# Turning from one batch to the next: a separate buffer for the first 64 tokens, no special order for the turning head

## The reference

```python
xn = _layernorm(x, axis=-1)
# attention
q = (x @ Wq + bq).reshape(b, h, t, dh)                        # no transpose of (t, h)
k = (x @ Wk + bk).reshape(b, t, h, dh).transpose(0, 2, 3, 1)
v = (x @ Wv + bv).reshape(b, t, h, dh).transpose(0, 2, 1, 3)
logits = jnp.einsum('bhtd,bhds->bhts', q, k) * scale
weights = jax.nn.softmax(logits + mask, axis=-1)
out = jnp.einsum('bhts,bhsd->bhtd', weights, v).transpose(0, 2, 1, 3).reshape(b, t, h * dh)
return out @ Wo + bo
# whole
x = x + attn(xn, ...) + ffn(xn, w_gate, w_shared_up, w_shared_down, w_up, w_down)
```

## Time and profile before

| | us |
|---|---|
| median of 3 runs | 1817.88 |
| lowest, highest of the 3 | 1813.98, 6824.79 |
| profiled execution, whole time | 1822.72 |
| its span, first to last instruction | 1821.0 |
| PE busy | 1690.2 (93% of the span) |
| DVE, POOL, ACT busy | 1368.7, 1122.1, 1085.7 |
| mean granted clock of PE | 0.956 of full speed |

### The profile page before, as it was taken

One profiled execution on the slowest core, in us unless ns is written; L12 is line 12 of the kernel. 1 busy time (PEld: TensorE's weight loads), 2 busy tenths in 40 slices (PEclk: granted clock), 3 DMA queues, 4 the chain that ended last, 5 costly groups with the idle time before them and its releaser, 6 DMA issues. The chain is left out here.

```text
span 1821.0 us, 49686 instructions
## 1 busy us (share of the span) xinstructions
PE 1690.2 (93%) x19217; PEld 1315.9 (72%) x19217; DVE 1368.7 (75%) x3128; ACT 1085.7 (60%) x2347; POOL 1122.1 (62%) x1006
## 2 busy tenths in 40 slices
PE   4699999999999999999986779999998999999997
PEld 3477767777777777777665667777776777777775
DVE  8677777777677777777663446888888888888885
ACT  2566666665566666666661227666666666666664
POOL 0257757776676777776660006777777677777763
PEclk7799999999999999999997669999999999999998
DMA  9377667765656665656656656778988789898976
GB/s 372 112 152 131 121 120 128 135 112 101 120 94 101 96 106 95 96 95 101 115 99 160 206 160 119 138 142 141 164 140 159 122 141 165 139 143 136 163 129 113
DMA packets 686658, 245.04 MB, mean 135 GB/s; under 512 B 637456, under 2 KB 674721, under 8 KB 685536
## 3 DMA queue, kind: packets, MB, share of 16 engines
q1 hardware_dynamic: 657472, 197.83, 61.6%
q0 software_dynamic: 18432, 33.64, 7.7%
q10 hardware_dynamic: 10528, 10.49, 1.8%
HBM read 57.11 MB, written 50.46 MB: 59 GB/s over the span
## 5 line engine op out<-in xcount | busy, mean ns | idle before, releaser
L485 POOL TENSOR_TENSOR prob<-prob 128x128 f16<-128x128 f32 (+7 forms) x512 | 653.0, 1280 | 576.1 <-ACT prob L874 569.2
L867 ACT ACTIVATE prob<-prob,nmax 128x128 f32<-128x128 f32 (+7 forms) x512 | 396.8, 775 | 530.4 <-DVE prob L1312 514.3
L708 PE MATMUL ps_s<-kT,qT 128*128 128x512 f16 (+3 forms) x2304 | 459.7, 327 | 4.3 <-DVE prob L1312 4.3
L723 PE MATMUL ps_o<-probT,vh 128*128 128x256 f16 (+1 forms) x3840 | 428.3, 265 | 7.2 <-DMA probT<-prob 7.2
L1312 DVE TENSOR_SCALAR_CACHE_REDUCE prob<-ps_s,neg_scale 128x128 f32<-128x128 f32 (+7 forms) x512 | 412.2, 809 | 14.3 <-PE ps_s L710 10.6
L723 PEld LDWEIGHTS ps_o<-probT,vh 128*128 128x128 f16 x3840 | 368.7, 99 | 53.5 <-issue 9.1
L874 ACT CAST prob<-prob 128x128 f16<-128x128 f32 (+7 forms) x512 | 341.5, 667 | 2.3
L708 PEld LDWEIGHTS ps_s<-kT,qT 128*128 128x128 f16 x2304 | 201.9, 98 | 144.7 <-issue 4.3
L1341 DVE SCALAR_TENSOR_TENSOR resid<-ps_y,yscale,resid 128x256 f32<-128x256 f32 x512 | 223.0, 477 | 11.6 <-PE ps_y L737 5.8
L737 PE MATMUL ps_y<-wo,oT 128*128 128x256 f16 x1536 | 210.6, 273 | 22.2 <-DVE oT L1327 20.4
L599 PEld LDWEIGHTS ps_t<-xT,wq 128*128 128x128 f16 x6144 | 205.1, 100 | 24.6 <-issue 9.8
(11 more groups left out here) (182 smaller groups left out, 1651.6 us busy)
## 6 DMA issues: line engine op xcount, KB each, us to landing
dispatched<-zeros SPq DMA_DIRECT2D x16, 512.0 KB, 14.1
probT<-prob SPq DMA_TRANSPOSE x512
ex<-dispatched SPq DMA_DIRECT2D x16, 512.0 KB, 4.3
expert_out<-eo ACTq DMA_DIRECT2D x16, 512.0 KB, 3.7
eup<-in_L_ffn_w_up_dram SPq DMA_DIRECT2D x64, 64.0 KB, 2.1
dispatched<-xn,slot_idx POOLq DMA_INDIRECT x192
xn_columns<-xnth SPq DMA_DIRECT2D x24, 128.0 KB
got<-expert_out,slot_idx POOLq DMA_INDIRECT x192
```

The source lines that it names most:

```text
L485: pool.tensor_tensor(low_cols(j), prob_cols(j).rearrange("p (r k) -> p r k", k=P), high_cols(j), ALU.subtract).then_inc(p_low, 1)
L708: pe.matmul(s_cols(j, lo, hi), qT[:, u, a, j * P:(j + 1) * P], kT[:, u, c, lo:hi], start=(n == 0), stop=(n == 2 and hi < w))
L723: mm = pe.matmul(ps_o[:, lo:2 * P], vh[:, u, a, r * D:(r + 1) * D], probT[:, PT_AT[c] + 2 * r + s, lo:], start=(r + n == 0), stop=(r == 2 ...
L867: nc.scalar.activation(prob_cols(j), prob_cols(j), ACT.Exp, bias=nmax[:, j:j + 1], scale=-1.0, accum_out=rsum[:, i % 2, j:j + 1]).then_inc ...
```

## The change

The order of the turning head is made that of every other head: `turn` and all its branches on PE, ACT and DVE are deleted. A buffer `xT_first` (64 KB) is added for the first 64 tokens of a batch. `load_first(b)` fills it with one DMA, listed on SP in the head before the turning one (14, 30, 46), between the transposes of block 6 and block 7. It waits for the stored columns of the batch and for the queries of the previous batch's first head, which were the last to read the buffer. The first queries of a batch read `xT_first` in place of `xT`. `load_xT` moves from ahead of block 1 to ahead of block 2 of the turning head, still waits for `v_done`, and brings all 1024 tokens in two halves of 512 (two DMAs of 256 KB each), each half with a semaphore of its own; each half of the first keys waits for its half of the tokens.

```diff
+            def load_first(b):
+                sp.wait_ge(xt_stored, 32 * NC * b)
+                sp.wait_ge(q_done, 2 * H * (b - 1) + 2)
+                sp.dma_start(xT_first[:], xnT_d[:, :, :, b * T:b * T + TPH]).then_inc(xT_head, 16)
+
             def load_xT(b):
-                sp.wait_ge(xt_stored, 32 * NC * b)
                 sp.wait_ge(v_done, 2 * H * b)
-                for n in range(2):
-                    sp.dma_start(xT[:, n, :, 0:TPH], xnT_d[:, n, :, b * T:b * T + TPH]).then_inc(xT_head, 16)
-                for n in range(2):
-                    sp.dma_start(xT[:, n, :, TPH:], xnT_d[:, n, :, b * T + TPH:(b + 1) * T]).then_inc(xT_in, 16)
+                for r in range(2):
+                    for n in range(2):
+                        sp.dma_start(xT[:, n, :, r * 512:(r + 1) * 512], xnT_d[:, n, :, b * T + r * 512:b * T + (r + 1) * 512]).then_inc(xT_in[r], 16)
...
                     for j in range(TB):
-                        if j == 1 and turn(i, i < B * H - 1):
+                        if j == TB - 1 and i % H == H - 2 and i < B * H - 2:
+                            load_first(i // H + 1)
+                        if j == 2 and i % H == H - 1 and i < B * H - 1:
                             load_xT(i // H + 1)
                         transpose_probs(i, j)
...
                 elif h == 0 and half == 0:
-                    pe.wait_ge(xT_head, 32 * (i // H))
+                    pe.wait_ge(xT_head, 16 * (i // H))
...
-                                           xT[:, c, k, h * TPH:(h + 1) * TPH], start=False, stop=(n + k == 3 and m % (H // 2) == H // 2 - 1))
+                                           xT_first[:, c, k, :] if i and h == 0 else xT[:, c, k, h * TPH:(h + 1) * TPH], start=False, stop=(n + k == 3 and m % (H // 2) == H // 2 - 1))
...
-                elif h == 0 and half == 0:
-                    pe.wait_ge(xT_in, 32 * (i // H))
+                elif i and h == 0:
+                    pe.wait_ge(xT_in[half], 32 * (i // H))
...
                     scores(i, 1)
-                    if turn(i, more):
-                        project_v(i, 0, more)
-                        project_v(i, 1, more)
-                    elif more:
+                    if more:
                         project_q(i + 1, 0)
                         project_q(i + 1, 1)
...
                     scores(i, 3)
-                    if turn(i, more):
-                        project_q(i + 1, 0)
-                        project_q(i + 1, 1)
-                    else:
-                        project_v(i, 0, more)
-                        project_v(i, 1, more)
+                    project_v(i, 0, more)
+                    project_v(i, 1, more)
```

More of the change, by code:

```diff
@@ L210, in causal_attention_with_moe @@
         xT_head = sem("xT_head")
-        xT_in = sem("xT_in")
+        xT_in = [sem(f"xT_in{n}") for n in range(2)]
         q_done = sem("q_done")
@@ L264, in causal_attention_with_moe @@
         xT = sb("xT", [P, 2, KC, T], F16)
+        xT_first = sb("xT_first", [P, 2, KC, TPH], F16)
         nmax = sb("nmax", [P, TB])
@@ L318, in late_part @@
             return i // 2 - 1 if i % 2 == 0 and 2 <= i <= ROWS else -1
-        def turn(i, more):
-            return more and i % H == H - 1
         def p_uses(i, j):
@@ L577, in project_q @@
                 elif h == 0 and half == 0:
-                    pe.wait_ge(xT_head, 32 * (i // H))
+                    pe.wait_ge(xT_head, 16 * (i // H))
                 if not fresh:
-                    if h == 0:
-                        pe.wait_ge(v_low, 2 * i - 1 + half)
-                    else:
-                        pe.wait_ge(k_low, 2 * i - 1 + half)
+                    pe.wait_ge(k_low, 2 * i - 1 + half)
                 if half == 0 and odd_part(i - 2) >= 0:
@@ L606, in project_k @@
                     pe.wait_ge(wsplit[1], 1)
-                elif h == 0 and half == 0:
-                    pe.wait_ge(xT_in, 32 * (i // H))
-                if fresh or h == 0:
+                elif i and h == 0:
+                    pe.wait_ge(xT_in[half], 32 * (i // H))
+                if fresh:
                     pe.wait_ge(q_low, 2 * i + half + 1)
@@ L629, in project_v @@
                     pe.wait_ge(wsplit[2], 1)
-                if more and not turn(i, more):
+                if more:
                     pe.wait_ge(q_low, 2 * i + half + 3)
@@ L647, in free_second_bank @@
             def free_second_bank(i):
[L648 to L651, removed]
+                pe.wait_ge(v_low, 2 * i + 2)
             def transpose_rows(i, p):
@@ L939, in attention @@
                     old, more = i > i0, i < i1 - 1
-                    swap = turn(i, more)
                     if odd_part(i) >= 0:
@@ L964, in attention @@
                     softmax_exp(i, 1)
[L965 to L968, removed]
+                    if more:
                         high_q(i + 1, 0)
                     high_probs(i, 1)
-                    if more and not swap:
+                    if more:
                         high_q(i + 1, 1)
@@ L979, in attention @@
                     softmax_exp(i, 3)
[L980 to L984, removed]
+                    high_v(i, 0)
+                    high_v(i, 1)
                     high_probs(i, 3)
-                    if swap:
-                        high_q(i + 1, 1)
                     softmax_exp(i, 4)
@@ L1373, in mixed @@
                         return max(0, min(NT * (TOPK + 1), TB * (i - i0) + j - MIX_LAG + 1)) if mixing else 0
-                    swap, even, odd, late = turn(i, more), even_part(i), odd_part(i), late_part(i)
+                    even, odd, late = even_part(i), odd_part(i), late_part(i)
                     block_max(i, 0)
@@ L1419, in attention @@
                         low_weights(2)
[L1420 to L1425, removed]
+                    low_v(i, 0)
+                    low_v(i, 1)
                     if odd >= 0:
```

## The result

| | before | changed |
|---|---|---|
| median, us | 1817.49 (6 runs) | 1826.29 (6 runs) |
| lowest and highest of the changed kernel's runs | | 1823.59, 1830.04 |
| ratio to before, 95% interval | | 1.0065 [1.0052, 1.0078] |
| profiled execution, us (span) | 1822.72 (1821.0) | 1830.04 (1828.3) |

The changed kernel is 0.65% slower. That is within the 2% band, but its 95% interval leaves out 1: some 9 us by the medians, 11.8 by the ratio, 7.3 between the two profiled executions. Measured again on another chip, in the last set of experiments, the ratio was 1.0067 [1.0049, 1.0086]. (One of the six runs of before took 6824.79 us and is no part of the ratio.)

What follows compares the result with a forecast made beforehand. PE, busy 93% of the span, was taken as the bound. Stalls of 17.5 us plus 6.1 for the clock against 15.5 before gave +8.1; +7 was taken, from 1817.9 to 1825, range 1813 to 1832, likeliest 1820 to 1829.

Steps and rivals of the forecast that it cites:

- Where PE asks, and where SP stands: First queries of a batch, after scores 1: SP issues the load 1.4 to 1.7 us after PE begins to wait.
- How long the load takes: Load of `xT_first` on SP's queue: stalls of 10.4 us as lower bound, 17.5 us as upper, the upper taken.
- the load's packets start only behind these: SP's queue: load moves after block 6's 448 KB transpose, needs another 1.3 us, lands at 465.1, 883.3 and 1402.3.
- The clock: Matmuls after each turn's stall run at a lower clock: 2.0 us each, 6.1 in all; 1.4 each for stalls of 3.4 to 3.6.
- The keys: First keys of the turning head: their half of the tokens lands 1.5 us before they ask, at no cost.
- The held transposes: SP holds transposes of blocks 2 and 3 behind the load of `xT`: hidden with 2 us to spare, no cost.
- The sum: Three turns: 15.5 us before, 23.6 after, +8.1 by the upper bound, −0.9 by the lower; +7 taken.
- The overtaking load: Rival on SP's queue: the load slips past the transpose, −0.9 us, 1817; chance 0.22.
- The early load: Rival at the turns: the load arrives before PE asks, turns become ordinary heads, −15.5 us, 1802; chance 0.06.
- The forecast's stall with a new one behind it: Rival: first keys or ACT's block 5 also wait, one to two us a turn, +10 to +14, about 1830; chance 0.12.

Runs made afterwards that it cites:

- e_early: Changed kernel with the 64-token load listed one head earlier on SP (heads 13, 29, 45), with the shorter wait for stored columns: 1805.99 us, 0.9924 of before.
- e_late: Changed kernel with the 64-token load one transpose later, behind that of block 7 of the head before the turning one: 1843.57 us in one run, 1.0133 of before.
- e_ahead: Changed kernel with the 64-token load issued just ahead of block 6's transpose, after the same wait for POOL: 1815.62 us in one run, against 1819.34 for before.
- e_otherqueue: Changed kernel with the 64-token load issued by ACT on its own DMA queue instead of SP's: 1815.48 us in one run, against 1815.81 for before.
- t_changed: The changed kernel again with nothing altered, measured on one chip beside three other kernels: 1824.31 us, 1.0067 of before.

## Why the prediction was right, point by point

- **Where PE asks, and where SP stands.** Right. I said 1.4 to 1.7 us from the ask to the issue; it was 1.8, 1.8 and 1.4. The stall moved from behind scores 3 to behind scores 1, and `e_early` shows that this placement is the whole of the loss.
- **How long the load takes.** The mechanism was right, its size too high. I let the load land when the transpose of block 6 had drained, 4.5, 4.7 and 3.9 us after issue; it took 3.34, 3.08 and 3.88. The step "the load's packets start only behind these" is what the packets did, in the three turns and again in `e_late`; on ACT's queue, where this order doesn't bind, they went among the transpose's. The 1.3 us from there to PE's start was 1.28, 1.08 and 1.58. What was mis-sized is the end of the transpose: I took 3.2, 3.4 and 2.6 us after the load's issue (463.8, 882.0 and 1401.0), and it was 2.06, 2.00 and 2.30 us. I had read these ends from the kernel before, 4.8, 5.0 and 4.1 us after the issue of block 6's transpose. In its first two turns the queue stood still for a while in between; the first one's window:

```profile
461.50:462.50 1.00, 1.00 (x15) 0.81 (x13) 0.93 (x5) 0.38 (x2) 0.95 (x1) 1.00 0.26 8
```

In the changed kernel no such pause fell into the transpose, and its last packet came 3.7, 3.6 and 3.7 us after its issue. Stalls: 15.3 us against 17.5 in the sum: the drain was 2.8 us too long in all, and the time from the ask to the issue 0.5 too short. On the Trainium skill: that descriptors of one ring are consumed in order ("DMA: Bandwidth & Descriptors", "Queues, rings and completion order") agrees with this trace, 1792 packets of the transpose and then the load's 512. The 2 us of fixed cost that the Trainium skill has on the same page ("Anatomy of one DMA — SWDGE (gpsimd) path", fitted there to DMAs that GpSimd issues; "Specifications" doesn't have it) are near the 2.3 to 2.5 us of `e_ahead`, where all that stood ahead had moved by the time of the load's first packet.
- **The clock.** Right in kind, with a term of 6.1 us. Against `e_early` the three heads cost 7.05, 6.42 and 8.07 us, of which 5.13, 4.88 and 5.26 + 0.96 were waits; 1.92 + 1.54 + 1.85 = 5.3 us are left for the slower clock and small differences. The 1.4 us that I put on a stall of 3.4 to 3.6 us are not settled: of the nearest waits, 3.83 and 3.77 us in `e_otherqueue`, one lost clock (0.94) and one didn't (1.00), and on one of 2.3 it is nothing.
- **The keys.** Costed at nothing; right in two turns, 0.96 us in the third. Issued from 1416.49, the first half let PE go on at 1422.44, 5.95 us later; I had 3.5 us after V. My rate of 274 GB/s was from the first turn; gathers of the experts' rows share the third, and I had the slack from head 30, before there are gathers. That this is the cause is not shown: in `t_changed`, with the same gathers, the third turn's keys didn't wait.
- **The held transposes.** Costed at nothing; in the third turn of the first profile ACT's high part of block 5 waited 1.5 us and head 48 took 1.0 us more. In `t_changed`, the same kernel, neither came again (head 48: 23.51 us). What decides it stays open.
- **The sum.** +7 forecast, +6.7 in the three turning heads (+5.6 in `t_changed`). The rest up to the 9 to 12 us of the runs is outside them: head 49 (24.1 us in both profiles, 23.33 before), in the first profile head 48, and head 51 at 1.3 us or more, which the forecast didn't have. So that 1825 lies so close to 1826.29 is partly luck: the stall was taken 2.2 us too long and the clock 0.8, and the effects behind the turn too short.
- **The rivals.** The overtaking load: no; in these runs the packets of load and transpose mixed only when they came from two queues (`e_otherqueue`). The early load: no. The forecast's stall with a new one behind it, given 0.12 at 10 to 14 us: the ratio's 11.8 us lies inside its numbers and not at my +7, but the waits it names came in one turn of one of the two profiles alone, and the larger part of what is missing is in head 51, which no rival had.

## What to carry to other kernels

A prefetch is as early as the last instruction ahead of it in the issuing queue, not as the loop index it is written under: find what that instruction waits for, and compare its time with the time at which the consumer asks. Here a transpose that waits for the end of a chain four engines long made "one head earlier" into 1.4 to 1.8 us late, and one line (H − 3 in place of H − 2, with the shorter wait for the columns that this place needs) turned +0.65% into −0.76%. When a change has several parts, try the one that removes the wait alone: the reordering brought nothing that the buffer didn't bring by itself. And a time from issue to landing can agree in two kernels by chance: before a queue's order is ruled out, look at when the packets moved.

## What the runs showed of the hardware that I had not expected

- A load of 64 KB took 2.3 to 2.5 us from issue to the waiting matmul when a transpose of 448 KB was issued behind it, 3.1 to 3.9 when the transpose was issued ahead of it in the same queue, and 3.5 to 4.1 when issued beside it from another engine's queue. In the same queue its packets moved behind the transpose's (from 460.89, the last of the transpose at 461.04), from the other queue among them (460.16 to 461.24, the transpose from 459.31 to 461.81), which brought PE's start 1.1 to 1.3 us nearer to the transpose's first packet.
- The same transpose of 448 KB took from issue to last packet 3.7 us in the first turn of the changed kernel and, with a pause of about 1 us in it, 4.4 in that of the kernel before (459.00 to 463.38).
- The issue itself also grew: 0.56 to 0.60 us on SP ahead of the transpose, 1.10 to 1.28 behind that of block 6, 0.88 to 1.10 behind that of block 7.
- A wait of PE of 2.3 to 2.4 us left the granted clock of heads 15 and 47 at 1.00, and so did one of 3.77 in head 31 of `e_otherqueue`; the kernel before lost clock after 3.14 and 3.23 us (0.94 both). The length of the wait alone doesn't tell. In the first turn of the changed kernel PE stood from 457.19, and the window from 460.5 shows the lower level, 1.2 GHz (0.50 of full speed):

```profile
460.00:460.50 0.50, 0.00 (x0) 0.00 (x0) 0.50 (x4) 0.00 (x0) 0.50 (x1) 0.91 1.13 200
460.50:461.00 0.50, 0.00 (x0) 0.00 (x0) 0.27 (x3) 0.46 (x2) 0.34 (x2) 0.50 0.96 173
```
